# Expert tiles in four groups, combination in the last steps, eight target slots, ScalarE's store of maxima, first-layer products behind blocks

## What is computed

```python
xn = layernorm(x)
# layer 0: attention without a softmax, and a feed-forward in blockwise 4-bit values
q, k, v = mlp(xn) for each of three small MLPs (gelu between two 128x128 products)
x = x + layernorm(tril(q @ k.T / scale) @ v) * ln_w + ln_b
      + fp4_linear(silu(fp4_linear(xn, w_gate)) * fp4_linear(xn, w_up), w_down)
xn = layernorm(x)
# layer 1: 16 heads of 64 with one shared key and value, and a mixture of 8 experts, 2 of them for a token
w = softmax((xn @ Wq + bq) @ (xn @ Wk + bk).T / 8)
attention = (w @ (xn @ Wv + bv)) @ Wo + bo
experts = sum over the 2 chosen experts of gate * (gelu(xn @ W1[e] + b1[e]) @ W2[e] + b2[e])
x = x + attention + experts
```

## Time and profile before

| what | us |
|---|---|
| three runs | 1475.42, 1468.08, 1470.13 (median 1470.13) |
| the profiled execution | 1460.9, of which the span of its instructions is 1459.0 |
| TensorE busy | 1300.1 (89% of the span) |
| VectorE busy | 1013.9 (69%) |
| ScalarE busy | 708.1 (49%) |
| GpSimd busy | 252.5 (17%) |

### The profile page before, as it was taken

How to read it: one execution, slowest core, us unless ns; L and a number is a source line. 1 busy time by engine, 2 the same in 40 slices (tenths; PEclk the granted TensorE clock), 3 DMA queues, 4 the chain that set the end, 5 groups by cost and what they waited for, 6 DMA issues and landing times.

```text
span 1459.0 us, 22233 instructions
## 1 busy us (share of the span) xinstructions
PE 1300.1 (89%) x7377; PEld 767.7 (53%) x7377; DVE 1013.9 (69%) x2393; ACT 708.1 (49%) x1300; POOL 252.5 (17%) x306
## 2 busy tenths in 40 slices
PE   4569888999999999999999999999998778979877
PEld 2335445555555555555555555555454466656634
DVE  7777776578757875787677767776776456666655
ACT  3136454544454445444545454545454464757531
POOL 3132222201010111011001200110002035242510
PEclk9579999999999999999999999999999899999989
DMA  2042442002000200020002000200003255445242
GB/s 72 14 130 93 128 139 103 31 17 77 24 29 17 82 22 26 17 82 24 24 17 82 26 23 17 82 27 21 16 18 113 78 167 171 135 157 163 72 154 59
DMA packets 72372, 100.26 MB, mean 69 GB/s; under 512 B 29196, under 2 KB 49228, under 8 KB 68292
## 3 DMA queue, kind: packets, MB, share of 16 engines
q1 hardware_dynamic: 59876, 70.69, 15.6%
q0 software_dynamic: 10192, 27.44, 5.8%
q10 hardware_dynamic: 2192, 0.71, 0.2%
HBM read 59.86 MB, written 38.68 MB: 68 GB/s over the span
## 4 chain that ended last, share of the span: by engine, by line
PE 61%; DVE 15%; issue 12%; POOL 6%; DMA 2%; SPq 2%; ACT 1%; DVEq 0%; POOLq 0%; ACTq 0%
PE bank L1423 13%; PE bank L1395 7%; PE bank L1351 6%; PE bank L1396 6%; PE bank L1434 6%; POOL y_rows L701 5%; PE bank L1455 4%; DVE mneg L990 3%; PE bank L1275 3%; PE bank L1259 3%; PE bank L1260 2%; PE bank L1261 2%; PE bank L1310 2%; DVE q_lm L984 2%; PE bank L1292 1%
## 5 line engine op out<-in xcount | busy, mean ns | idle before, releaser
L821 ACT ACTIVATE wide<-bank 128x512 f32<-128x512 f32 x512 | 301.5, 604 | 502.8 <-PE bank L1396 492.5
L990 DVE TENSOR_REDUCE mneg<-bank 128x1 f32<-128x512 f32 x512 | 347.4, 686 | 203.6 <-PE bank L1351 197.7
L1395 PE MATMUL bank<-q_hh,k_hl 128*128 128x512 f32 x512 | 236.2, 461 | 19.8 <-DMA q_lm<-mrow 18.2
L1423 PE MATMUL bank<-wide,v_w 128*32 128x512 f32 x2048 | 248.7, 604 | 0.5 <-issue 0.5
L1351 PE MATMUL bank<-k_hl,q_hh 128*128 128x512 f32 x512 | 208.5, 409 | 36.0 <-DVE mneg L990 22.1
L1396 PE MATMUL bank<-q_lm,k_h 65*128 65x512 f32 x512 | 204.2, 399 | 0.0
L1395 PEld LDWEIGHTS bank<-q_hh,k_hl 128*128 128x128 f32 x512 | 97.7, 191 | 151.6 <-issue 109.4
L1351 PEld LDWEIGHTS bank<-k_hl,q_hh 128*128 128x128 f32 x512 | 98.7, 193 | 73.7 <-issue 52.8
L631 POOL TENSOR_TENSOR rs<-rs,power 128x4 f32<-128x4 f32 x24 | 24.6, 1026 | 626.2 <-DVE rs L892 626.2
L1434 PE MATMUL bank<-wide,ones 128*32 128x512 f32 x992 | 129.1, 592 | 0.0
L701 POOL DMA_INDIRECT y_rows<-y_m,to_u x92 | 92.4, 1004 | 177.0 <-DVE y_m L1117 155.0
(11 more groups left out here) (230 smaller groups left out, 2001.4 us busy)
## 6 DMA issues: line engine op xcount, KB each, us to landing
w_t<-w_rows SPq DMA_DIRECT2D x23, 1024.0 KB
x_rows<-part_h POOLq DMA_DIRECT2D x65, 258.0 KB, 5.7
inv<-inverse_scratch SPq DMA_DIRECT2D x124, 128.0 KB, 3.0
w_rows<-w_t SPq DMA_DIRECT2D x8, 1024.0 KB, 4.9
x_m<-x_rows SPq DMA_DIRECT2D x23, 258.0 KB
stage<-in_L_ffn_W SPq DMA_DIRECT2D x16, 256.0 KB, 4.8
yab<-y_rows SPq DMA_DIRECT2D x8, 512.0 KB, 7.3
xin<-in_L_attn_x SPq DMA_DIRECT2D x8, 256.0 KB, 4.0
```

What stands on the lines that cost most here:

```text
L821: act.activation(wide[:, st.g % WIDE, :], ps, ACT.Exp, scale=SCALE1).then_inc(wide_full, 1)
L990: dve.tensor_reduce(mneg[:, (gh // 2) % 2, col:col + 1], ps[:], X, ALU.max, negate=True)\
L1395: pe.matmul(ps, k_hl[:, n, t], q_hh[:, gh % HEADS, :], start=True, stop=False)
L1423: pe.matmul(ps_out[0][rows, :], v_w[:, n, c, TILE * d:TILE * d + TILE], weights, start=(c == 0), stop=(c == TT - 1))
```

## The change

Six edits. (1) The expert tiles stand in four groups of 6, 6, 6 and 5 behind k = 15, 23, 31 and 39, and the 16 combination pieces at k = 53 to 61, two at most steps. (2) The targets have eight slots (TO) with eight semaphores, so `tile_in` of tile t waits for tile t - 8; y_m keeps three slots. Rows are turned at the first step of a tile's place instead of the second, results at the third. (3) ScalarE starts the 4 KB transfer of the maxima itself, right behind its copy, and waits for that copy first; GpSimd starts the eight loads of yab behind its last scatter. The loads of the first four tiles' weights are spread over k = 1, 5, 10 and 13. (4) All first-layer products stand at k % 4 = 1, behind `values`. For that, xq and xqt get memory of their own (in part_h), and VectorE's pieces are placed anew. (5) The query product stands ahead of the maxima's at its step, and VectorE's q_lm ahead of the first-layer pieces. (6) GpSimd's two inverse roots in row 0 stand three and one places earlier among the weight splits.

```diff
-    WT, XT, YT, YM = 4, 2, 2, 3
-    INSERT = {15: 8, 23: 8, 31: 7}
+    WT, XT, YT, YM, TO = 4, 2, 2, 3, 8
+    INSERT = {15: 6, 23: 6, 31: 6, 39: 5}
-    L0_AT = {1: -8, 2: -7, 3: -5, 4: -5, 5: -3, 6: -2, 7: -1, 8: -1, 9: 1, 10: 2, 13: 2, 14: 3, 15: 4, 16: 4,
-             17: 8, 19: 16, 20: 17, 21: 24, 22: 25, 23: 32, 24: 33, 25: 38, 26: 39, 27: 41}
+    L0_AT = {1: -7, 2: -7, 3: -3, 4: -3, 5: 1, 6: 1, 13: 1, 14: 1, 7: 5, 8: 5, 9: 9, 10: 9, 15: 13, 16: 13, 17: 13,
+             19: 17, 20: 17, 21: 25, 22: 25, 23: 33, 24: 33, 25: 37, 26: 37, 27: 41}
-    L0_DVE = [-14, -11, -11, -10, -7, -6, -4, -2, 0, 0, 9, 10, 13, 17, 18, 21, 25, 26, 29, 30, 30, 31, 32,
-              33, 34, 37, 38, 39, 40, 42, 43, 44, 44]
+    L0_DVE = [-14, -11, -11, -10, -8, -6, -5, -2, 2, 6, 14, 14, 15, 18, 19, 20, 21, 22, 23, 24, 26, 27, 29, 31,
+              34, 34, 35, 38, 40, 42, 43, 44, 44]
-    LANDED_AT = 41
-    COMBINE_AT = [46 + 2 * n for n in range(NB)]
+    ROWS_AT, WEIGHTS_AT = 10, [1, 5, 10, 13]
+    COMBINE_AT = [53 + n for n in range(NB)]
...
+        here, c = divmod(st.g, TT)
+        use, i = {0: ("tx", here + 1), 2: ("ty", here - 2)}.get(c, (None, None))
+        return [(use, tile_of[i])] if i in tile_of else []
...
+        if s % TT == 1 and 0 <= ahead_ + 1 < H * NB:
+            events.append(("q", ahead_ + 1))
         if 0 <= ahead_ < H * NB:
             events.append(("mx", ahead_, s % TT))
         if s == TT + 1 and 0 <= gh + 2 < H * NB:
             events.append(("mt", (gh + 2) // 2))
-        if s % TT == 1 and 0 <= ahead_ + 1 < H * NB:
-            events.append(("q", ahead_ + 1))
...
-            eng.wait_ge(y_scattered[t % WT], TT * (t // WT + 1) * 16)
+            eng.wait_ge(y_scattered[t % TO], TT * (t // TO + 1) * 16)
...
-                for event in head_events(st):
-                    if event[0] == "mt":
-                        store_m(event[1])
...
-                    if st.kind == "o" and st.k == 0:
                         for i in range(WT):
                             sp.wait_ge(w_stored[i], E // WT * 16)
-                        for t in range(WT):
-                            load_tile_weights(t)
-                    if st.kind == "o" and st.k == 9:
+                    if st.kind == "o" and st.k in WEIGHTS_AT:
+                        load_tile_weights(WEIGHTS_AT.index(st.k))
+                    if st.kind == "o" and st.k == ROWS_AT:
...
-                if SPLIT_STEPS[j] in (33, 48):
+                if SPLIT_STEPS[j] in (24, 45):
                     root()
...
+            for t in range(TILES - TO, TILES):
+                landed(pool, t)
+            for n in range(NB):
+                pool.dma_start(yab[:, n], y_rows[1 + 2 * S * n:1 + 2 * S * (n + 1), :]
+                               .rearrange("(i p b) d -> p i b d", p=P, b=2)).then_inc(yab_loaded[n], 16)
...
                 act.activation(mrow[:, pair % 2, :], ps[0:2 * TT, 0:P], ACT.Identity).then_inc(free, 1)
+                read_out(act, ("mt", pair))
+                at_ = (2 * pair) % HEADS
+                act.dma_start(q_lm[DK:DK + 1, at_:at_ + 2, :].bitcast(F32), mrow[:, pair % 2, :].bitcast(F32))\
+                   .then_inc(m_loaded[pair % 2], 16)
...
-                if t >= WT:
-                    landed(dve, t - WT)
+                if t >= TO:
+                    landed(dve, t - TO)
...
             for st in steps:
+                if split_head(st) is not None:
+                    lo_q(split_head(st))
                 if st.kind in ("pre", "o"):
                     for n, k in ((st.r + 1, st.k), (st.r + 2, st.k - ATT)):
                         for _ in range(L0_DVE.count(k) if 0 < n < NB else 0):
                             next(cuts[n], None)
-                if split_head(st) is not None:
-                    lo_q(split_head(st))
```

More of the change, by code:

```diff
@@ L194, in tile_events @@
     def tile_events(st):
-        if st.g is None or st.g % TT != 1:
+        if st.g is None:
             return []
-        here = st.g // TT
-        return [(use, tile_of[i]) for use, i in (("tx", here + 1), ("ty", here - 2)) if i in tile_of]
+        here, c = divmod(st.g, TT)
+        use, i = {0: ("tx", here + 1), 2: ("ty", here - 2)}.get(c, (None, None))
+        return [(use, tile_of[i])] if i in tile_of else []
     def row_steps(st):
@@ L325, in two_layers @@
         hid0, s0t, sg = over("hid0", [P, 3, S], 1), over("s0t", [P, TT, S], 1), over("sg", [P, TT, I0], 1)
-        qk0, xq, xqt = over("qk0", [P, 2, S], 5), over("xq", [P, S], 5), over("xqt", [P, S], 6)
+        qk0 = over("qk0", [P, 2, S], 5)
         hqt = over("hqt", [P, 2, IC, P], 4)
@@ L374, in two_layers @@
         b_t = sb("b_t", [P, WT, 8])
[L375 to L376 removed]
+        to_f, to_u = sb("to_f", [P, TT]), sb("to_u", [P, TO, TT], U32)
         bank = [ctx.enter_context(nc.psum_tensor(f"bank{i}", [P, S], F32)) for i in range(8)]
@@ L548, in load_tile_rows @@
                   .then_inc(xm_loaded[t % XT], 16)
-            def load_landed(n):
-                if n == 0:
-                    for t in range(TILES - WT, TILES):
-                        landed(sp, t)
-                sp.dma_start(yab[:, n], y_rows[1 + 2 * S * n:1 + 2 * S * (n + 1), :]
-                             .rearrange("(i p b) d -> p i b d", p=P, b=2)).then_inc(yab_loaded[n], 16)
             def store_out(n):
@@ L922, in l0 @@
                 last_product = next(quantise)
+                if n > 0:
+                    yield last_product
+                    for _ in quantise:
+                        pass
                 yield 6
@@ L935, in l0 @@
                                              SCALE0, causal[:], ALU.mult, ALU.mult).then_inc(free, 1)
-                yield last_product
-                for _ in quantise:
-                    pass
+                if n == 0:
+                    yield last_product
+                    for _ in quantise:
+                        pass
                 def down(i):
@@ L948, in attended, with gain @@
                     yield from norm(v0, v0, link, tag)
+                def gain():
+                    link(dve.tensor_tensor(v0[:], v0[:], wide_(lnw_row), ALU.mult))
+                    link(dve.tensor_tensor(v0[:], v0[:], wide_(lnb_row), ALU.add))
                 if n == 0:
@@ L962, in l0 @@
                     yield from fp4(sg[:, i, :], sg[:, i, :], NBI, lambda ins: ins.then_inc(hq_done, 1), (s, s, None))
+                    if i == 1 and n > 0:
+                        yield from attended(s)
                     if i == 2 and n > 0:
-                        yield from attended(s)
-                yield 24
-                link(dve.tensor_tensor(v0[:], v0[:], wide_(lnw_row), ALU.mult))
-                link(dve.tensor_tensor(v0[:], v0[:], wide_(lnb_row), ALU.add))
+                        yield s
+                        gain()
+                if n == 0:
+                    yield 24
+                    gain()
                 yield 26
@@ L1106, in tile_in @@
                 dve.tensor_tensor(xt_l[:, i, :], ps[:], xt_h[:, i, :].bitcast(F32), ALU.subtract).then_inc(free, 1)
-                if t >= WT:
-                    landed(dve, t - WT)
+                if t >= TO:
+                    landed(dve, t - TO)
                 target = x_m[:, t % XT, :, P]
                 link(dve.scalar_tensor_tensor(to_f[:], target, 0.0, spare[:, t, :], ALU.is_equal, ALU.mult))
-                dve.tensor_tensor(to_u[:, t % WT, :], to_f[:], target, ALU.add).then_inc(to_set, 1)
+                dve.tensor_tensor(to_u[:, t % TO, :], to_f[:], target, ALU.add).then_inc(to_set, 1)
             def tile_turned(t):
```

26 lines of the change are left out of this document (12 added, 14 removed).

## The result

The changed kernel takes 1492.4 us (median of four runs, 1489.1 to 1494.3), the kernel before 1471.0 in the same comparison: a ratio of 1.014, 95% interval 1.011 to 1.017. It is slower by 1.4%, where I forecast 6% faster.

The account below looks back on a forecast made before the run. TensorE was taken to bound the middle rows, scatter and maxima waits the last. 40 + 22 + 6 + 27 - 1.5 - 3 = 90.5 us off the profiled 1460.9, plus 9.2 to the median, gave 1380; range 1352 to 1415.

Parts of the forecast that it names:

- Base of the sum: Whole kernel: 1370.4 us from the profiled 1460.9, plus 9.2 by which the median of runs lies above the profiled execution.
- Eight slots: Last row: VectorE's waits for scatters to land go and TensorE sets the tile; 40 us won.
- The store leaves SP: Last row: TensorE's waits of 11.35 and 6.82 us for the maxima's transfer go, with their low clock; 22 us won.
- Roots: Row 0: GpSimd's root one split earlier ends VectorE's 6.72 us wait and TensorE's behind it; 6 us won.
- Four groups and the late combination: Last row: one more group entry costs 1.5 us, a longer wait at the last projection 3.
- Middle rows: Rows 1 to 6: moving first-layer products and the query nets 4.5 us a row, 27 for six rows.
- Removed, 9.0 a row: Middle rows: TensorE's 5.7 us of waits, 1.7 of low clock and some 1.6 of passages between products go.
- Tables, 1.9: Middle rows: ScalarE's table changes, no longer hidden, make TensorE wait 1.2 us at stage 3 and 0.7 at stage 15.
- VectorE's cluster, 2.6: Middle rows, steps 14 to 24: VectorE has 22.9 us of work against TensorE's 19; cost put at 2.6 a row.
- Clock: Middle rows: each wait at stage 3 is followed by 3.4 us of lower clock; the 1.7 us lost goes.
- VectorE sets the middle rows: Rival: VectorE's cluster and the tables eat the 9.0 a row, last row as forecast; 1407 us, chance 0.20.
- ScalarE's store alone: Rival, slower: the store's wait and start hold ScalarE, 62 times; at 5.2 us each, 1492 us; chance 0.03.

Follow-up runs that it names:

- e3: The kernel before with eight target slots and nothing else; 1431 us.
- e1: The changed kernel with the first-layer part alone undone (products, VectorE's pieces, query and q_lm order as before); 1414 us.
- e10: e1 with SP loading the first two tiles' rows at step 5 of the last row instead of 10; 1405 us.
- e13: e1 with three groups of expert tiles (8, 8, 7) and the combination at steps 46, 48 and on, as before; 1411 us.
- e9: e8 with quantisation of the next row's input and of the last up product also spread to later steps; 1461 us.
- e12: e9 with the three hidden products and their gelus at step 59, in the stream, instead of 61; 1443 us.
- e8: The changed kernel with VectorE's three pieces for the first up product moved from steps 14, 14, 15 to 17; gave 15 us back.
- e6: e1 with both orders kept: query product ahead of the maxima's, q_lm ahead of VectorE's first-layer pieces; 1421 us.
- e11: e1 with q_lm ahead of VectorE's first-layer pieces, nothing else; 1410 us.
- e16: e15 with the query's product behind maximum and transposition again; 1430 us.
- e15: e12 with VectorE's read of the second up product moved from step 18 to 19; 1442 us.
- e7: The changed kernel with the query's product behind maximum and transposition again; gave 7 us.
- e5: The kernel before with the store of maxima started by ScalarE instead of SP, nothing else; gave 10 us.

## Why the prediction was wrong, by its own steps

**Base of the sum.** I added 9.2 us from the profiled execution to the median. Of the sixteen other kernels ten have their median within 1 us of their profiled execution, and the farthest is 5 above. The profiled execution of before is the fastest of over thirty (the others took 1464 to 1476), and its mean clock, 0.953, is as high as that of any. So it was a lucky one. It matters for one reading: by the traces the slots gained 29 us (spans of 1459.0 and 1429.9), by the medians 40.

**Eight slots: 40, measured 40.** Right by the medians. By the traces it is 29, against the lucky execution of before: the 28.2 that TensorE waited for part_l are gone, with 8.5 us of lost clock in the last part (23.9 before, 15.4 in e3), and e3 has 4.7 us of new waits whose cause its trace does not name.

**The store leaves SP: 22, measured 10.** The mechanism was right and the size wrong. I wrote that the 11.35 is one wait of SP's program, and gave all of it to the maxima. But the exchange of the sums and the rows for the first tiles stand in the same program. They were late before too, hidden under the longer wait, and kept 5.08 and 3.69 us of it. I did not ask what was late next. On e1, whose spread weight loads leave no wait for the sums, moving the rows (e10) brought another 9.4.

**Roots: 6, measured about 4 to 5.** From the start to row 0's step 54, e1 takes 226.9 for 231.6; the wait for the root is 0.53 for 6.72. No run had the roots alone. I had also written that the other root was not waited for. It was, for 1.20 us at 172.32, and so was a third, 5.18 us at 230.18 of before, which stands behind eight transfer starts in GpSimd's order:

```profile
224.69 4.40 POOL L659 DMA_DIRECT2D x_rows<-part_h  x8
229.11 1.04 POOL L631 TENSOR_TENSOR rs<-rs,power 128x4 f32<-128x4 f32 x1
```

```profile
230.18 0.16 DVE L896 SCALAR_TENSOR_TENSOR rs<-rs 128x4 f32<-128x4 f32 x1 [5.18 <-POOL rs L631]
```

TensorE waits 3.90 us behind it, at the projection of step 54. No kernel here touched it, and it stands at 225.48 in e1 as it was.

**Four groups and the late combination: -4.5, measured -3.4** (e13, within the noise). TensorE's wait at the last projection but one is 1.89 in e1, 0.63 in e13.

These four make 63.5 in the sum, and all but the first-layer part together measured 57 (e1).

**Middle rows: 27 won, measured 64 lost in the six rows and 78 with row 0 and the end.** This is the step that failed: the sum of 9.0 - 1.9 - 2.6 a row, in it above all the 2.6 for VectorE, which I took from comparing sums of work, and the low clock that comes, which I put at nothing. Its parts:
- *Removed, 9.0 a row.* The six waits went. The 1.6 for passages did not: a row of e9 in which the clock costs the same 1.7 as before keeps TensorE busy 140.0 us for 137.9.
- *Tables, 1.9.* The waits are 1.29 and 0.48 for my 1.2 and 0.7. ScalarE starts an exponential in the instant the load ends, as in the earlier trace rows. The drain of about 1.38 us that the Trainium skill adds to a load (ScalarE: Activation LUTs, What ACT_TABLE_LOAD costs) shows neither before nor behind it in this trace, and my waits without it fit. Without the longer wait (e12) a row is 4.0 shorter, of which 1.8 are waits; the rest is clock, for a reason that stays open.

```profile
880.95 0.69 ACT L718 ACTIVATE hid<-bank,b 128x512 f32<-128x512 f32 x1 [0.17 <-PE bank L1282]
881.65 1.28 ACT L816 ACT_TABLE_LOAD   x1
882.95 1.08 ACT L816 ACTIVATE wide<-bank 128x512 f32<-128x512 f32 x2
```

- *VectorE's cluster, 2.6.* I compared sums: 22.9 us of work in steps where TensorE has 19, so late by 4. But VectorE does not work through a sum. It stands still, 4.1 and 6.9 us, in front of up products that now come later, and what stands behind them in its order is late: on 2.5 and xres 1.8 a row. Moving only when it reads the first of them gave 15 us back (e8). The other waits stand behind its own pieces, placed too close: mneg 1.8 behind the quantisation of the last up product, and q_lm 2.2 at rk behind 7 us in which VectorE never pauses. Spreading pieces there gave 16 more and took the first away, not the second (e9).
- *Clock.* I counted stretches of low clock that go (1.7 a row) and none that come. They cost 8.5 us in 740 before and 22.2 after. One of them, behind the wait at rk:

```profile
869.50 0.38 PE L1387 MATMUL bank<-picked_t,before 128*128 128x32 f32 x2 [2.20 <-DVE q_lm L991]
...
871.05 0.63 PE L1403 MATMUL bank<-q_lm,k_h 65*128 65x512 f32 x1
```

- *The query ahead* I set out with no price. It costs 11 and 12 (e6 against e11, e16 against e15), outside the middle rows in the first pair; the 7 of e7 is not clear of the noise.

The rival *VectorE sets the middle rows* had the right mechanism, and its 1407 was wrong since it let the rows fall no lower than where they were. None of my cases had VectorE make these rows longer. That is also why my chance for slower was 0.03: I looked for it at ScalarE's store alone. That rival's figure, 1492, is the measured one by luck: it asked for starts of 5.2 us, and they took 0.63 and left the middle rows of e5 at 143.8.

**What stays open.** Of the 78 us, the pieces account for 31 (e8, e9) and 1 (e15), the tables' place with its clock for 18 (e12), the query for 12 (e16). The 20 us between e16 (1430) and e11 (1410) are the remaining placement, with 6.9 us of waits a row for 4.3; they were not taken apart further. With the 4.6 that lo_q ahead gains on the other side (e11), these make the 78. Open too are the wait at rk, which none of the moves of pieces took away, and what decides whether a short wait is followed by low clock.

## What to carry to other kernels

When a producer's instruction is moved later, look first at where its reader stands in its own engine's order: a reader that comes early idles, and everything queued behind it is late by as much, whatever the engine's average load says. When a wait in an in-order queue is removed, read on in that queue to what comes next, and price only the difference. And when a schedule is credited with the low clock that goes with the waits it removes, look also for the low clock that its new waits may bring.

## What the runs showed of the hardware

TensorE's clock made over a quarter of the loss in the middle rows. They had 6.3 us more idle time each, in waits of 0.3 to 2.5 us, and lost 13.7 us more in 740 (2.9 a row) to the lower level, 1.2 GHz. The sum of the waits does not settle it: in these 740 us e6 lost 1.7 with 5.3 to 6.0 us of waits in a row, e11 10.2 with 4.3, e12 8.5 with 6.4, and the kernel before 8.5 with 5.6. Between executions of one kernel the mean clock goes with the time too: the kernel before took 1460.9 us at 0.953 and 1475.5 at 0.943.
